# Last product: 127 rows by GpSimd's indirect transfer, the row of the last partition by SyncE

## What is computed

```
# layer 1 (gated): norm, two products over the edges, gates, residual, layer norm
h  = batchnorm(x) * gamma + beta
a_in  = segment_sum((h @ W_in  + b_in )[src] * iw[:, None], dst)
a_out = segment_sum((h @ W_out + b_out)[dst] * ow[:, None], src)
g  = gates(concat(a_in, a_out) @ W_x2i + b_x2i, h @ W_h2h)
x1 = layernorm(x + g)
# layer 2: normalise columns, one product over the edges, a linear map, residual, layer norm
f   = (x1 - mean(x1, 0)) / (std(x1, 0, ddof=1) + 1e-4)
out = layernorm(x1 + segment_sum(edge_weight[:, None] * f[src], dst) @ weight + bias)
```

## Time and profile before

| | us |
|---|---|
| median of 3 runs | 3405.44 (3403.34 to 3405.46) |
| the profiled execution | 3413.44 |
| its span, first to last instruction | 3411.7 |
| GpSimd busy in the span | 2529.2 (74%) |
| TensorE busy in the span | 2507.6 (73%) |
| VectorE busy in the span | 2299.3 (67%) |

### The profile page before, as it was taken

One profiled execution on the slowest core, in us unless ns is written; L12 is line 12 of the kernel. 1 busy time (PEld: TensorE's weight loads), 2 busy tenths in 40 slices (PEclk: granted clock), 3 DMA queues, 4 the chain that ended last, 5 costly groups with the idle time before them and its releaser, 6 DMA issues.

```text
span 3411.7 us, 47557 instructions
## 1 busy us (share of the span) xinstructions
PE 2507.6 (73%) x10659; PEld 1840.3 (54%) x10701; DVE 2299.3 (67%) x5450; ACT 1059.9 (31%) x3135; POOL 2529.2 (74%) x2706
## 2 busy tenths in 40 slices
PE   5776766666676666579999999996776665556777
PEld 4555544444344443368888888543444444444565
DVE  7989977777777677657776777786455455555455
ACT  3344333333333333245555555562000000000022
POOL 6777677777777777777777777576777777777775
PEclk8878988888988889799999999998988888887899
DMA  6554344444444444388988999454333333333344
GB/s 163 157 147 126 120 158 154 158 162 155 157 155 156 163 155 156 129 262 285 289 288 284 291 290 292 153 172 136 105 105 105 105 105 105 105 105 106 109 137 120
DMA packets 275056, 565.29 MB, mean 166 GB/s; under 512 B 55599, under 2 KB 121126, under 8 KB 274787
## 3 DMA queue, kind: packets, MB, share of 16 engines
q0 software_dynamic: 119808, 329.02, 30.8%
q1 hardware_dynamic: 146452, 223.99, 20.8%
q10 hardware_dynamic: 8528, 9.30, 0.9%
HBM read 419.19 MB, written 142.88 MB: 165 GB/s over the span
## 4 chain that ended last, share of the span: by engine, by line
POOL 49%; PE 22%; issue 18%; DVE 7%; DMA 2%; ACT 1%; DVEq 1%; SPq 0%; POOLq 0%; ACTq 0%
POOL arena L630 23%; POOL messages L560 21%; PE ps L1152 11%; PE ps L962 8%; POOL arena L554 5%; PE ps L1185 2%; PE ps L1085 1%; DMA messages<-arena 1%; DVE ps L2037 1%; DVE ps L2036 1%; DMA arena<-messages 1%; ACT arena L739 0%; DVE bn L2018 0%; DVE ps L1605 0%; DVE ps L1606 0%
## 5 line engine op out<-in xcount | busy, mean ns | idle before, releaser
L560 POOL DMA_INDIRECT messages<-arena x832 | 803.8, 966 | 264.1 <-issue 249.0
L554 POOL DMA_INDIRECT arena<-in_x,arena x832 | 792.1, 952 | 272.3 <-issue 250.7
L630 POOL DMA_INDIRECT arena<-x_table,wh x832 | 790.0, 950 | 263.2 <-issue 253.4
L1222 PE MATMUL ps<-arena 128*128 x2048 | 603.0, 450 | 367.0 <-SPq L505 366.7
L1222 PEld LDWEIGHTS ps<-arena 128*128 128x128 f32 x2048 | 439.4, 223 | 536.6 <-issue 469.8
L962 PE MATMUL ps<-arena 128*128 128x128 f32 x3328 | 457.8, 296 | 127.6 <-ACT arena L676 89.9
L739 ACT ACTIVATE arena<-ps,arena 128x256 f32<-128x256 f32 x832 | 326.5, 475 | 703.3 <-PE ps L1085 466.0
L962 PEld LDWEIGHTS ps<-arena 128*128 128x128 f32 x3328 | 436.8, 209 | 193.1 <-ACT arena L676 128.9
L1085 PE MATMUL ps<-arena 128*128 128x256 f32 x1664 | 470.7, 434 | 49.6 <-DVE arena L1789 42.2
L2212 DVE TENSOR_TENSOR node_a<-node_a,ps 128x256 f32 x256 | 107.7, 421 | 503.7 <-PE ps L1222 501.6
L1085 PEld LDWEIGHTS ps<-arena 128*128 128x128 f32 x1664 | 364.2, 221 | 78.9 <-issue 23.9
(11 more groups left out here) (287 smaller groups left out, 2981.9 us busy)
## 6 DMA issues: line engine op xcount, KB each, us to landing
arena<-messages SPq DMA_DIRECT2D x464, 260.0 KB
arena<-in_x SPq DMA_DIRECT2D x304, 128.0 KB, 2.8
gate_rows<-arena SPq DMA_DIRECT2D x49, 384.0 KB, 2.4
arena<-gate_rows SPq DMA_DIRECT2D x49, 384.0 KB, 3.0
arena<-in_x,arena POOLq DMA_INDIRECT x832
messages<-arena POOLq DMA_INDIRECT x832, 2.5
arena<-x_table,wh POOLq DMA_INDIRECT x832, 2.8
arena<-in_x SPq DMA_DIRECT2D x48, 256.0 KB, 2.9
```

The source lines that it names most:

```text
L554: nc.gpsimd.indirect_dma_start(out=big[:, s, j, 0:D], out_offset=None, in_=x, in_offset=bass.IndirectOffsetOnAxis(ap=ids[:, j:j + 1], axis ...
L560: nc.gpsimd.indirect_dma_start(out=messages, out_offset=bass.IndirectOffsetOnAxis(ap=ids[:, j:j + 1], axis=0), in_=big[:, s, j, :], in_off ...
L630: nc.gpsimd.indirect_dma_start(out=last_rows[:, (g + 1) % LAST_ROWS, j * D:(j + 1) * D], out_offset=None, in_=x1_table, in_offset=bass.Ind ...
L1222: last = nc.tensor.matmul(ps[g % LAST_SUMS][:, 0:D], last_hot[h][:, j, :], last_rows[:, bass.ds(k, 1), j * D:(j + 1) * D].rearrange("p o d ...
```

## The change

GpSimd's indirect transfers of the last product get 127 partitions in place of 128 (`BY_POOL = P - 1`). The row of partition 127 is fetched by SP with an ordinary DMA of one row, four for each group. For that, SP copies the row numbers of partition 127 (832 integers) into partition 0 (`late_row`), since it reads its registers from there, and issues the four DMAs of a group three groups ahead of the group that it handles. It reads the four row numbers first and then issues the four DMAs. It waits for their landing as well before it raises `second_landed`. The semaphores of the early loads of x are used a second time for it and renamed.

```diff
+BY_POOL = P - 1
...
+        late_row = area(hot_at + 3840, [GATHERED * CPG], I32)[0:1, :]
...
             for t in range(3 * SPAN):
                 gates_load(t, t % GATES)
+            sp.wait_ge(S["back_kept"], 2 * PAIRS)
+            sp.wait_ge(S["back_mm"], 2 * PAIRS)
+            sp.dma_start(late_row, back_id[BY_POOL:P, 0:GATHERED * CPG]).then_inc(S["row_back"], 16)
...
+            def last_row(g):
+
+                ids = [nc.sync.value_load(late_row[0:1, g * CPG + j:g * CPG + j + 1]).with_bounds(min_val=0, max_val=NT * P - 1)
+                       for j in range(CPG)]
+                for j in range(CPG):
+                    sp.dma_start(last_rows[BY_POOL:P, (g + 1) % LAST_ROWS, j * D:(j + 1) * D],
+                                 x1_table[bass.ds(ids[j], 1), :]).then_inc(S[f"rows_loaded{g % RING}"], 16)
+
+            sp.wait_ge(S["row_back"], 32)
+            sp.wait_ge(S["x1_stored"], 16 * (SPANS + 1))
+            for g in range(RING - 1):
+                last_row(g)
             for g in range(GATHERED):
                 sp.wait_ge(S[f"second_rows{g % LAST_ROWS}"], (g // LAST_ROWS + 1) * 16 * CPG)
+                sp.wait_ge(S[f"rows_loaded{g % RING}"], 16 * (2 * XPAIRS // RING + (g // RING + 1) * CPG))
                 sp.sem_inc(S["second_landed"], 1)
...
+                if g + RING - 1 < GATHERED:
+                    last_row(g + RING - 1)
...
                     nc.gpsimd.indirect_dma_start(
-                        out=last_rows[:, (g + 1) % LAST_ROWS, j * D:(j + 1) * D], out_offset=None, in_=x1_table,
-                        in_offset=bass.IndirectOffsetOnAxis(ap=back_id[:, g * CPG + j:g * CPG + j + 1], axis=0)).then_inc(S[f"second_rows{k}"], 16)
+                        out=last_rows[0:BY_POOL, (g + 1) % LAST_ROWS, j * D:(j + 1) * D], out_offset=None, in_=x1_table,
+                        in_offset=bass.IndirectOffsetOnAxis(ap=back_id[0:BY_POOL, g * CPG + j:g * CPG + j + 1], axis=0)).then_inc(S[f"second_rows{k}"], 16)
```

More of the change, by code:

```diff
@@ L377, in x_load @@
                 sp.dma_start(xs[:, s, :].rearrange("p (t d) -> p t d", t=2),
-                             x[2 * q * P:(2 * q + 2) * P, :].rearrange("(t p) d -> p t d", p=P)).then_inc(S[f"xs_loaded{s}"], 16)
+                             x[2 * q * P:(2 * q + 2) * P, :].rearrange("(t p) d -> p t d", p=P)).then_inc(S[f"rows_loaded{s}"], 16)
             sp.dma_start(xt[0:TAIL, :], x[FULL * P:N, :]).then_inc(S["xt_loaded"], 16)
@@ L972, in x_sum @@
             def x_sum(i, s):
-                pe.wait_ge(S[f"xs_loaded{s}"], 16 * i)
+                pe.wait_ge(S[f"rows_loaded{s}"], 16 * i)
                 nc.tensor.matmul(ps[0][:, :], ones[:, :], xs[:, s, :], start=isinstance(i, int) and i == 1 and s == 0, stop=False).then_inc(S["x_used"], 1)
@@ L1479, in run @@
                 def run():
-                    dve.wait_ge(S[f"xs_loaded{s}"], 16 * (i - X_SHIFT + XPAIRS // RING + 1))
+                    dve.wait_ge(S[f"rows_loaded{s}"], 16 * (i - X_SHIFT + XPAIRS // RING + 1))
                     mean = ps[0][:, 0:D].rearrange("p (o d) -> p o d", o=1).broadcast_to([P, 2, D])
```

## The result

| | before | after |
|---|---|---|
| median, us | 3405.45 (3403.34 to 3406.19, 4 runs) | 4740.3 (4737.71 to 4742.97, 4 runs) |
| ratio | | 1.3916, 95% interval 1.3899 to 1.3932 |
| profiled execution, span | 3411.7 | 4738.0 |

The forecast was 3308 us, faster. The time went the other way and lies far outside the range.

A forecast was written before the change was run, and what follows sets the result against it. GpSimd's own pace in the last product's transfers was taken as the bound. Against the median, 3405.4 - 104 (transfers) + 6.2 (landing at the end) = 3307.6, say 3308 us; SP's work added nothing; range 3165 to 3450.

The forecast's parts named there:

- What bounds the kernel: Last product's stage: GpSimd's own pace sets it, 1.254 us a transfer, 5.02 us a group of four; it never waits for slots.
- GpSimd's transfers: L630: 127 rows take 0.87 of 949 ns, so 824 ns, pause unchanged; the stage loses 104 us.
- rival C: L630: an uneven transfer is dearer for GpSimd, 1.31 x 949 = 1245 ns, +246, with the end 3658 us; chance 0.14.
- The landing: Last product's transfers: 127 rows on one engine land up to 6.2 us later, hidden inside the stage, +6.2 us at its end.
- SP's new work: SP in the last product: 0.79 us a row, 3.95 us a group with the old part, under 5.02, so costs nothing.
- The rest of the edit: SP's new gates-stage wait, its DMA, the three groups issued ahead of the loop and renamed semaphores: no term in the sum.
- B: GpSimd's transfers: time by rows or fixed, like a fixed program, nothing saved that counts; 3399 to 3412 us, chance 0.18.
- D: SP becomes the bound in the last product: 1.23 us a row, 5.72 a group, +146, with the end 3557 us; chance 0.08.
- the second rule that I weighed: GpSimd's descriptor generation: small, many emitted before a further one costs; rows save nothing and the end gives 3412 us.
- E: Last product: every 127-row transfer goes to the same engine, 5533 us in place of 1042, 7900 in all; chance 0.04.

## Why the prediction was wrong

- **What bounds the kernel: right.** The stage followed GpSimd's pace transfer for transfer, before and after.
- **GpSimd's transfers: wrong, and this step is the error: 1428 of the 1432 us between forecast and measurement.** I priced an uneven count by SP's issues, 0.76 to 1.31 times an even one, and took 0.87. It is 2541 / 949 = 2.68 times. The term was forecast at -104 us and measured 831 x 1.594 = +1324. The bounds were too narrow because they came from another engine's way of dealing out rows, in which nothing shows a filling up; the direction was that of rival C, whose 1245 ns for a transfer was half of what came. No row of before could have shown it: where 16 divides the rows, 48 packets come out with filling and without. I took from them that 127 rows would go to one engine, which the packet sizes bear out, and did not ask what the other 15 lists would look like. That left 0.87 without a row of GpSimd's behind it, and the prediction calls it the most in doubt.
- **The landing: right, but not by the row's 7.9 us.** That median can't be set beside 2.8. It counts from the start of GpSimd's instruction, now 1.6 us longer, and the four transfers of a group count on one semaphore, so that early counts of the next transfer, 2.8 us later, are taken for the last ones of this one. Taken apart by place in the group, the trace has 7.9 us for the first three transfers and 10.4 for the fourth, which has no next one; before it was 2.7 to 2.8 for all four. Of the fourth's +7.6 us 1.6 are the instruction, and 6.0 are left of the forecast 6.2. It is hidden inside the stage (GpSimd's only waits are "issue") and moves the end: +6.2 forecast, +7.0 measured from the last transfer to the end, 1.6 of them from the longer instruction, which was no part of this term.
- **SP's new work: right.** I took 0.79 us a row. SP's work done twice gives 0.76, and the run with 128 rows shows it hidden, 1.0003. SP's work done twice, at 6.89 us a group, shows SP taking over; where between the two the bound lies, 5.02 us by the prediction, was not measured.
- **The rest of the edit: right**, by the same run with 128 rows.
- **Rivals.** C came in direction, not in size. B's "fixed program" is nearly true for even counts: 838 ns remain at 16 rows. D did not come either: SP's new work was hidden. Of the second rule that I weighed (the Trainium skill, "DMA: Bandwidth & Descriptors", section "Anatomy of one DMA — SWDGE (gpsimd) path", by which many descriptors can be emitted before more of them cost), the runs show that at 128 entries their share is small, by the formula some 107 of 949 ns, though not nothing (112 rows were 17 us faster), and that it does not hold at 2032, where the entries are 1699 of 2541 ns. E did not come: with every transfer on the same engine the 832 would have needed 5533 us by the prediction's rate, and the stage took 2367.
- **Open:** counts with k from 3 to 15 cost 16 to 31 ns above the formula, and 112, 96 and 16, which 16 divides, 12 to 17 below it. No run looked into that, nor into what GpSimd does with each entry. Scatters with an uneven count were not tried.

## What to carry to other kernels

Give GpSimd's indirect transfers a row count that 16 divides, and if it can't be, one with a large divisor up to 16: the price follows 842 + 0.836 x 16 n / k ns here (n rows, k the largest number up to 16 that divides n; within 3.3%), so 126 or 120 rows cost little more than 128 and 127 or 113 cost more than twice as much. Cutting rows is no way to speed such a stage up; some 840 of 949 ns do not depend on them. And when an edit changes the shape of an operation that sets the pace, a price from another engine is no bound; such a term is measured by itself first.

## What the runs showed of the hardware that was not expected

- Empty entries: a GpSimd transfer whose rows fall on one engine still puts as many entries on each of the other 15, with 4 bytes each, 1905 of them for 127 rows.
- SP's register loads from the arena took 451 ns in the median beside the 127-row transfers and 269 beside the 128-row ones, the same instruction on the same data. The first line is of the changed kernel, to be set beside L511 above; the cause was not looked into.

```profile
L510 SPq TENSOR_LOAD <-arena x832: 261/451/1707, 2342.1 to 4686.7; - x167
```

- An SP DMA of one row of 1 KB takes 218 ns to issue here, against 333 for 128 rows; the one-row issue at L370 took 289.
